# A recurrent kernel whose engine loops get other bounds: TensorE 513 steps, VectorE rounds of 32, another preamble order

## What is computed

```python
vz, vr, vh = cond @ C_z + b_z, cond @ C_r + b_r, cond @ C + b
xz, xr, xh = x @ W_z, x @ W_r, x @ W            # for all 512 steps
h = 0
for t in range(512):
    z  = sigmoid(xz[t] + h @ U_z + vz)
    r  = sigmoid(xr[t] + h @ U_r + vr)
    hh = tanh(xh[t] + (r * h) @ U + vh)
    h  = (1 - z) * h + z * hh
    out[t] = x[t] + h
```

## Time and profile before

| | us |
|---|---|
| median of 3 executions | 2266.47 (2265.84 to 2267.73) |
| the profiled execution | 2264.97 |
| span of its profile | 2263.1 |
| TensorE matmul busy | 2185.4 (97%) |
| VectorE busy | 1754.5 (78%) |
| ScalarE busy | 1326.6 (59%) |
| GpSimd busy | 687.8 (30%) |

### The profile page before, as it was taken

One profiled execution on the slowest core, in us unless ns is written; L12 is line 12 of the kernel. 1 busy time (PEld: TensorE's weight loads), 2 busy tenths in 40 slices (PEclk: granted clock), 3 DMA queues, 4 the chain that ended last, 5 costly groups with the idle time before them and its releaser, 6 DMA issues.

```text
span 2263.1 us, 238050 instructions
## 1 busy us (share of the span) xinstructions
PE 2185.4 (97%) x107502; PEld 1797.5 (79%) x107502; DVE 1754.5 (78%) x8226; ACT 1326.6 (59%) x4623; POOL 687.8 (30%) x1546
## 2 busy tenths in 40 slices
PE   2899999999999999999999999999999999999996
PEld 1788878888888887888888888788878888888875
DVE  5687878778778777777777777777777877877874
ACT  3566556566566665666656666556656656656652
POOL 0233333333333333333333333333333333333331
PEclk9999999999999999999999999999999999999998
DMA  9110110110110110111101101101101101101101
GB/s 196 34 38 19 38 38 19 38 37 19 38 33 23 38 35 22 38 29 28 38 24 33 38 24 32 38 19 37 38 19 38 38 19 38 38 20 38 28 11 22
DMA packets 145390, 78.48 MB, mean 35 GB/s; under 512 B 9024, under 2 KB 140608, under 8 KB 145216
## 3 DMA queue, kind: packets, MB, share of 16 engines
q1 hardware_dynamic: 145216, 76.84, 14.1%
HBM read 43.25 MB, written 33.55 MB: 34 GB/s over the span
## 4 chain that ended last, share of the span: by engine, by line
PE 95%; issue 2%; SPq 1%; DMA 1%; DVE 0%; ACT 0%; DVEq 0%; POOLq 0%; POOL 0%
PE p_bank L269 44%; PE c_bank L259 20%; PE banks L297 16%; PE banks L306 15%; SPq L152 1%; DMA x_nat<-in_x_dram 1%; SPq L147 0%; SPq L163 0%; PE p_bank L278 0%; DVE taken L631 0%; DVE state L635 0%; DVE h_t L639 0%; ACT gate_c L430 0%; SPq L155 0%; DVE h_lo L597 0%
## 5 line engine op out<-in xcount | busy, mean ns | idle before, releaser
L269 PE MATMUL p_bank<-w_hi,x_t 128*32 128x384 f16 x16384 | 1183.1, 327 | 2.4 <-issue 1.6
L269 PE MATMUL p_bank<-w_lo,x_t 128*32 128x384 f16 x8192 | 701.7, 327 | 2.2 <-issue 2.2
L269 PEld LDWEIGHTS p_bank<-w_hi,x_t 128*32 128x32 f16 x16384 | 462.3, 97 | 155.2 <-issue 1.5
L259 PEld LDWEIGHTS c_bank<-u,reset_t 128*32 128x32 f32 x32704 | 488.4, 110 | 98.6 <-DVE reset_t L611 71.7
L259 PE MATMUL c_bank<-u,reset_t 128*32 128x64 f32 x32704 | 551.0, 219 | 8.4 <-issue 8.1
L230 POOL TENSOR_TENSOR result<-x_nat,state 128x128 f32<-128x128 f32 x512 | 233.9, 457 | 1010.0 <-DVE h_lo L597 1008.4
L423 ACT ACTIVATE gate_r<-banks,gates_down 128x64 f32<-128x64 f32 x1024 | 265.6, 310 | 359.1 <-PE banks L297 358.1
L430 ACT ACTIVATE gate_c<-c_bank 128x64 f32<-128x64 f32 x1024 | 228.3, 223 | 302.8 <-PE c_bank L259 302.6
L216 POOL TENSOR_TENSOR kept<-keep,state 128x128 f32<-128x128 f32 x512 | 235.7, 460 | 551.3 <-ACT keep L426 551.3
L609 DVE TENSOR_TENSOR reset<-gate_r,state 128x64 f32<-128x64 f32 x1024 | 209.0, 204 | 209.3 <-ACT gate_r L423 205.8
L419 ACT ACTIVATE h_hi<-h_t 128x64 f16<-128x64 f32 x1024 | 261.0, 255 | 148.0 <-DVE h_t L639 80.4
(11 more groups left out here) (68 smaller groups left out, 2749.6 us busy)
## 6 DMA issues: line engine op xcount, KB each, us to landing
x_nat<-in_x_dram SPq DMA_DIRECT2D x256, 128.0 KB, 3.1
out_dram<-result SPq DMA_DIRECT2D x256, 128.0 KB, 2.8
w_stage<-in_L_cond_W_r_dram SPq DMA_DIRECT2D x4, 256.0 KB, 5.4
w_stage<-in_L_cond_W_z_dram SPq DMA_DIRECT2D x4, 256.0 KB, 8.1
w_stage<-in_L_cond_W_dram SPq DMA_DIRECT2D x4, 256.0 KB, 10.8
u<-in_L_cond_U_z_dram SPq DMA_DIRECT2D x4, 256.0 KB, 13.5
u<-in_L_cond_U_r_dram SPq DMA_DIRECT2D x4, 256.0 KB, 16.0
c_w<-in_L_cond_C_r_dram SPq DMA_DIRECT2D x4, 256.0 KB, 12.7
```

The source lines that it names most:

```text
L259: last = nc.tensor.matmul(c_bank[part(j), a, 0:N // HALVES], reset_t[:, part(q)], u[:, C, q, half_cols(j, a)], start=False, stop=q == Q - ...
L269: last = nc.tensor.matmul(p_bank[k][part(j), 0:G * N], x_t[:, c, part(q), a], w[b][:, :, q, cols(j)], start=f == 0, stop=f == GROUPS - 1, ...
```

## The change

TensorE's loop now has 128 passes of four steps, from step 1 to step 512. Step 512 doesn't exist in the recurrence: its products are made from what lies in the tiles and nobody reads them. So that its waits are met, VectorE and ScalarE add to the semaphores at their ends, and ScalarE and VectorE also count up where they used to leave out a sum or a turn. Steps 510 and 511 now also make projections that nobody reads. VectorE's loop has 15 passes of 32 steps with 32 written out behind it. In the preamble W_r is loaded first, cond after W_h; VectorE takes the maximum of W_r before it waits for the sums of x, and turns cond later; ScalarE's sum of the third set comes behind its step 0, TensorE's total of it behind the projection for step 2; TensorE waits for U_h before step 1; and SyncE issues x blocks 2 and 3 once two results are out.

```diff
--- before.py
+++ after.py
@@ -32,6 +32,8 @@
     PARTS = ((0, 0), (0, 1), (1, 0))
     GROUPS = Q * len(PARTS)
     BEFORE_C = 3
+    OUT_BEFORE_X = 2
+    ROUND = 32
     POW = 14
     LEAST = 2.0 ** -60
     SETS = T // SET
@@ -151,11 +153,12 @@
                 for p in range(J):
                     sp.dma_start(tile[part(p)], rows[p]).then_inc(done, 16)
 
+            load_weights(w_stage[:, R], W_r, s_w_in[R])
+            load_x(0, 0)
+            load_weights(w_stage[:, Z], W_z, s_w_in[Z])
+            load_weights(w_stage[:, C], W_h, s_w_in[C])
             for p in range(J):
                 sp.dma_start(cond_nat[part(p)], cond[:, cols(p)]).then_inc(s_cond_in, 16)
-            load_x(0, 0)
-            for g, m in enumerate((W_r, W_z, W_h)):
-                load_weights(w_stage[:, g], m, s_w_in[g])
             load_weights(u[:, Z], U_z, s_u_in[Z])
             load_weights(u[:, R], U_r, s_u_in[R])
             for g, b in enumerate((b_r, b_z, b_h)):
@@ -165,7 +168,7 @@
                 load_weights(c_w[:, g], c, s_c_in[g])
             load_x(1, 1)
             load_weights(u[:, C], U_h, s_u_in[C])
-            sp.wait_ge(s_u_in[C], 16 * J)
+            sp.wait_ge(out_ready, OUT_BEFORE_X)
             for n in range(2, BUFS):
                 load_x(n, n)
 
@@ -337,42 +340,32 @@
             pe.sem_inc(r_mm, 1)
             pe.sem_inc(z_mm, 1)
             pe.sem_inc(c_mm, HALVES)
-            total_x(TOTAL_STEP % 2, 0, 0, 3)
             pe.wait_ge(x_t_ready, 3)
             project(0, 2, 0, GROUPS)
-            def step(m, tt, last, candidate_in=None):
+            total_x(TOTAL_STEP % 2, 0, 0, 3)
+            pe.wait_ge(s_w_hi, len(SPLITS))
+            pe.wait_ge(s_w_lo, len(SPLITS))
+            pe.wait_ge(s_u_in[C], 16 * J)
+
+            def step(m, tt):
                 s = m * SET + tt
                 c, k = tt % SET, tt % 2
-                fill = not (last and s >= T - 2)
-
-                def count(v):
-                    return v if last else pe.snap(v)
-
-                now = count(s + 1)
-                halves = [count(HALVES * s + (a + 1)) for a in range(HALVES)]
+                now = pe.snap(s + 1)
+                halves = [pe.snap(HALVES * s + (a + 1)) for a in range(HALVES)]
                 pe.wait_ge(seeded, now)
                 reset_product(cell(k, R), halves).then_inc(r_mm, 1)
                 update_product(cell(k, Z)).then_inc(z_mm, 1)
                 pe.wait_ge(c_seeded, now)
-                if fill:
-                    if c == TOTAL_STEP and not (last and m + tt // SET >= SETS - 2):
-                        total_x(TOTAL_STEP % 2, 0, 0, count(m + (tt // SET + 3)))
-                    pe.wait_ge(x_t_ready, count(s + 3))
-                    project(k, (c + 2) % SET, 0, BEFORE_C)
-                if candidate_in is not None:
-                    pe.wait_ge(candidate_in, 16 * J)
+                if c == TOTAL_STEP:
+                    total_x(TOTAL_STEP % 2, 0, 0, pe.snap(m + (tt // SET + 3)))
+                pe.wait_ge(x_t_ready, pe.snap(s + 3))
+                project(k, (c + 2) % SET, 0, BEFORE_C)
                 candidate_product([(reset_t_ready, a) for a in halves])
-                if fill:
-                    project(k, (c + 2) % SET, BEFORE_C, GROUPS)
-
-            pe.wait_ge(s_w_hi, len(SPLITS))
-            pe.wait_ge(s_w_lo, len(SPLITS))
-            step(0, 1, True, s_u_in[C])
-            with pe.Fori(0, SETS - 3) as m:
-                for tt in range(2, SET + 2):
-                    step(m, tt, False)
-            for s in range(SET * (SETS - 3) + 2, T):
-                step(s // SET, s % SET, True)
+                project(k, (c + 2) % SET, BEFORE_C, GROUPS)
+
+            with pe.Fori(0, SETS) as m:
+                for tt in range(1, SET + 1):
+                    step(m, tt)
 
         @block.scalar
         def _(act):
@@ -404,9 +397,6 @@
                 act.wait_ge(s_w_up, k + 1)
                 nc.scalar.activation(split_of(g, 0), stage_of(g), ACT.Copy, scale=w_up[:, k:k + 1]).then_inc(s_w_hi, 1)
             nc.scalar.activation(table[:], w_up[:, 0:1], ACT.Sigmoid)
-            act.wait_ge(x_in[1], 16 * J)
-            act.wait_ge(x_summed, 2)
-            sum_x(2, 0)
             act.wait_ge(s_gates_scale, 1)
 
             def step(i, tt, last, first=False):
@@ -437,6 +427,12 @@
 
                 m, t = divmod(tt, SET)
                 now_m = i * (STEPS // SET) + m
+                if first and tt == 0:
+                    act.wait_ge(x_in[1], 16 * J)
+                    act.wait_ge(x_summed, 2)
+                    sum_x(2, 0)
+                if t == SUM_STEP and not more(3):
+                    act.sem_inc(x_summed, 1)
                 if t == SUM_STEP and more(3):
                     act.wait_ge(x_totaled, count(now_m + 3))
                     if (m + 3) % 2 == 0:
@@ -459,6 +455,7 @@
                     step(i, tt, False)
             for tt in range(SET, STEPS):
                 step(PASSES - 1, tt, True)
+            act.sem_inc(h_hi_ready, HALVES)
 
         @block.vector
         def _(dve):
@@ -538,8 +535,7 @@
                                      ALU.mult))
                 dve.sem_inc(s_gates_scale, 1)
 
-            dve.wait_ge(s_cond_in, 16 * J)
-            V.transpose(cond_t[:], cond_nat[:]).then_inc(s_cond_t, 1)
+            top_of_w(R)
             dve.wait_ge(x_totaled, 2)
             for m in range(2):
                 power_x(m, p_bank[1][:, G * N + m:G * N + m + 1], m, int)
@@ -547,11 +543,12 @@
                 up_x(m, m, int)
             for c in range(TURN_AHEAD):
                 turn_x(0, c, SET)
-            top_of_w(R)
             top_of_w(Z)
             scale_of_w(W_GATES)
             top_of_w(C)
             scale_of_w(W_C)
+            dve.wait_ge(s_cond_in, 16 * J)
+            V.transpose(cond_t[:], cond_nat[:]).then_inc(s_cond_t, 1)
             rest_of_w(0)
             rest_of_w(1)
             top_of_w(UZ)
@@ -579,9 +576,9 @@
             dve.wait_ge(s_bits, 6)
 
             def step(i, tt, last):
-                s = i * STEPS + tt
+                s = i * ROUND + tt
                 m, t = divmod(tt, SET)
-                now_m = i * (STEPS // SET) + m
+                now_m = i * (ROUND // SET) + m
                 old, new = state[:, (tt - 1) % SLOTS], state[:, tt % SLOTS]
 
                 def count(v):
@@ -590,7 +587,7 @@
                 now = count(s + 1)
 
                 def more(sets):
-                    return not (last and m + sets >= STEPS // SET)
+                    return not (last and m + sets >= ROUND // SET)
 
                 for a in range(HALVES):
                     dve.wait_ge(h_hi_ready, count(HALVES * s + (a + 1)))
@@ -612,7 +609,7 @@
 
                 if t == POWER_STEP and more(2):
                     least_x(m % 2, now_m + 2, count)
-                if not (last and tt == STEPS - 1):
+                if not (last and tt == ROUND - 1):
                     if t == SET - 1:
                         dve.wait_ge(x_down_ready, count(now_m + 2))
                     dve.wait_ge(projected, count(s + 2))
@@ -620,7 +617,9 @@
                 if t == POWER_STEP and more(2):
                     up_x(m % 2, now_m + 2, count)
                 dve.wait_ge(kept_ready, now)
-                if not (last and tt >= STEPS - TURN_AHEAD):
+                if last and tt >= ROUND - TURN_AHEAD:
+                    dve.sem_inc(x_t_ready, 1)
+                else:
                     ahead_m, c = divmod(tt + TURN_AHEAD, SET)
                     turn_x(ahead_m % 2, c, count(s + (TURN_AHEAD + 1)))
 
@@ -645,11 +644,15 @@
                 renew(1)
                 turn(1)
 
-            with nc.Fori(0, PASSES - 1, engines=[dve.engine], hint_back_edge=True) as i:
-                for tt in range(STEPS):
+            with nc.Fori(0, T // ROUND - 1, engines=[dve.engine], hint_back_edge=True) as i:
+                for tt in range(ROUND):
                     step(i, tt, False)
-            for tt in range(STEPS):
-                step(PASSES - 1, tt, True)
+            for tt in range(ROUND):
+                step(T // ROUND - 1, tt, True)
+            dve.sem_inc(seeded, 1)
+            dve.sem_inc(c_seeded, 1)
+            dve.sem_inc(h_lo_ready, HALVES)
+            dve.sem_inc(reset_t_ready, HALVES)
 
 
 # ---- launch: one core; inputs and output as the reference has them ----
```

## The result

The changed kernel takes **4062.1 us** (median of 4; 4058.7 to 4067.5) against 2266.15 (2265.5 to 2267.7): ratio 1.7925, 95% interval 1.7894 to 1.7957. The forecast was 2754, its range 2250 to 3050. The direction and the place of the loss were right; its size lies nearest to that of the rival with everything thrown out (14%, about 4350). The profiled execution took 4058.7 us.

What follows compares the result with a forecast made beforehand. The prediction took TensorE to bound the kernel at 4.235 us a step. From the profiled 2265.0 us, parts of -7.3 and +495 for refetching the loop head's block gave 2752.7, as a median about 2754 us; range 2250 to 3050.

Steps and rivals of the forecast that it cites:

- the rival with everything thrown out: TensorE's loop: store refilled in turn, nine blocks a pass at 3.7 us each, about 4350 us; chance 14%.
- Where the time is now: TensorE bounds the loop at 4.235 us a step; fresh code costs about 1.8 more, as does each VectorE back edge.
- The parts: Whole kernel without eviction: the change's separate gains and costs sum to -7.3 us, median 2259.2; chance 33%.
- Tail and last step: End of run: steps 502 to 511 from TensorE's resident loop, -16.3 us; last step at the loop's pace, -2.8.
- Step 512: TensorE's extra step at the end finishes slightly later than the old span's end: +0.4 us for the barrier.
- Start: Before step 1: VectorE's seed, then held by the clearing of banks, comes 1 us earlier and TensorE's total moves: -1.4 us.
- First pass: TensorE's first steps: four instead of five run on fresh code, -1.6 us.
- VectorE's loop: Rounds of 32 steps: 14 back edges in place of 6, each stalling 1.8 us, +14.4 us.
- The 14 stalls: Sign on VectorE: 14 stalls of 1.5 us, some 167 us apart; fewer would refute the count of its blocks.
- The place of TensorE's loop: TensorE's 1697-instruction loop touches seven instruction blocks before, eight after the change, and then asks for a ninth.
- The head alone is the forecast: TensorE's back edges: only the loop head's block is thrown out, 127 waits of 3.9 us, +495 us; chance 48%.

Runs made afterwards that it cites:

- the moved loop: Changed kernel with the head of TensorE's loop laid on the first slot of a 256-instruction block: 2257.8 us, ratio 0.9965.
- the hinted one: Changed kernel with a hint for the branch back added to TensorE's loop, its place unchanged: 2258.1 us, ratio 0.9967.
- the mended kernel: Changed kernel with TensorE's loop at a block's start (2257.8 us) or its back edge hinted (2258.1); the former with VectorE's rounds of 64 again: 2245.45 us.

## Why the prediction was wrong, point by point

**Where the time is now** held: steps of 4.235 us, resident code, 1.8 us a step for fresh code, 1.6 to 1.8 at each back edge.

**The parts** held together. Without the refetching the kernel is 2257.8 where they gave 2259.2, span 2255.3, 7.8 below the old, where the sum was 7.3. One by one, from the chain and timeline of the kernel with the moved loop and the hinted one:

- Tail and last step (-16.3, -2.8): the nine steps from 502 to 511 take 38.1 us where they took 54.4, 4.23 each with no stall, and from the start of step 511 to the result row pass 3.82 us, as worked out (3.8):

```profile
2246.54 0.70 PE banks L300 x48
```

```profile
2250.36 0.46 POOL L233 TENSOR_TENSOR result<-x_nat,state 128x128 f32<-128x128 f32 x1 [1.49 <-DVE state L634]
```

- Step 512 (+0.4): the span ends 4.9 us after that row, as before: 0.
- Start (-1.4): step 1 starts at 54.82 in the changed kernel where it was 55.98: -1.2. The size was right by luck, for the way was not. C_h landed 1.5 us earlier, at 45.54, though the bytes ahead of it were the same, and what then held the seed was no clearing of banks but a wait for instructions of 2.2 us, ended by VectorE's entry into its loop:

```profile
28.60 16.94 DMA c_w<-in_L_cond_C_dram
45.54 0.04 issue
...
48.12 2.22 issue
50.34 3.41 PE p_bank L272 x44
```

- First pass (-1.6): from step 1 to step 6 it took 83.64 - 53.93 = 29.7 us in the hinted kernel against 29.4: nothing gained. Of the stalls, single ones of 1.9 and 1.75 us are longer than the longest before, 1.3. The moved kernel needed 28.8, with its first step at the 1.2 GHz level. Of this term 0.6 came in the one kernel and nothing in the other.
- VectorE's loop (+14.4): +12.7 alone, 12.3 in the mended kernel; 1.6 a back edge in place of 1.8. The 14 stalls that the prediction named as a sign stand in the mended kernels; in the changed one the longer passes swallow them.

**The place of TensorE's loop** held: seven blocks before with almost no room, eight after, a ninth asked for.

**The step that failed** is "The head alone is the forecast": that only the pair of clashing blocks would be lost, at 3.9 us for each of 127 back edges. The runs show nine packets in each pass in place of two: the store is refilled in turn, and each pass costs 31.3 us in place of 16.94, 14.37 more. 127 x 14.37 = 1825; less the 23 us of VectorE's 14 stalls, which only the mended kernel pays, that is 1802 of the 1804 us that separate the two. The pause at the edge measured 3.9 us, the price that the sum had, but for other reasons. The sum took 3.3 us from the request to the next instruction and 0.6 for the clock. In the trace before, the packet starts at 2198.20, 1.0 us after the entry that was taken for the request, and the next instruction comes 2.3 us later; and in the changed kernel two packets go out ahead of the pause, and the low clock comes on top. The 3.9 was luck, and the pause is only the first of a pass's waits. The rival that had this was priced at nine blocks of 3.7 us; they took 3.48 on average, so 4062 in place of 4350. I gave it 14% because placing by address seemed the simpler store; no row spoke for that. The range stopped at 3050 and left out the one case for which a row (the rate in the written-out steps) gave a price.

The Trainium skill, Runtime: NRT & Kernel Launch, Instruction fetch mechanics, calls this memory a first-in, first-out store; the nine packets a pass agree with that (as they would with throwing out the block used longest ago), and by it the rival at about 4350 would have been the forecast. Eight blocks of 16 KB, its 128 KiB, is what the pair of the hinted loop (eight held) and the unhinted one (nine asked for, all lost) shows here.

## What to carry to other kernels

When a loop's code nearly fills what its engine can hold, count its instructions and where it starts, and count the block behind it too: sixteen instructions of shift cost a third here and a hundred a factor of 1.8, and a hint on the back edge or a fixed slot for its head made it safe here at no measurable cost on TensorE. A mechanism found in the trace isn't priced until it is known what it does to its neighbours; where two ways of replacement differ by a factor, both belong in the range. For a loop whose code isn't held, what counts is how far ahead of the branch the head's block is asked for, and each back edge has a plain price besides, if nothing covers the engine there.

## What the runs showed that I had not expected

- A loop that touches eight blocks by 9 or 41 instructions is refilled in every second pass only (584 packets, 3064 and 3094 us), one by 91 in every pass (1142 packets, 4024 us).
- A back edge of VectorE costs TensorE's step 0.32 us even when no wait for instructions is left at it.
- Laying VectorE's loop at a chosen slot cost 4.3 us once at the entry; 24 memsets that do run, in a time of waiting, cost nothing there.
- In the changed kernel TensorE's next block is asked for not on entering a block but some time later, in the median 1.1 us.
